# Mixture-of-experts front stage on one core: where z's scale and bias come from, and in what order its inputs are loaded

## What is computed

```
x_filtered = ifft(fft(x_quat, axis=1) * spectral_gate).real       # the gate is one factor per channel
x_rotated  = hamilton(normalize(cond), hamilton(x_filtered, conj(normalize(q_right))))
t      = x_rotated @ W_in + b_in
probs  = softmax(t @ W_gate + b_gate); topv, topi = top_k(probs, 2); topv = topv / sum(topv)
mid    = relu(einsum('nd,edh->neh', t, W1) + b1)                   # 8 experts, 256 -> 1024
eout   = einsum('neh,ehd->ned', mid, W2) + b2                      # 1024 -> 256
out    = x + (sum over the 2 choices of route * eout) @ W_out + b_out
```

## Time and profile before

| | |
|---|---|
| median of 3 runs | 515.55 us |
| the profiled execution | 515.1 us, of which the span of the profile is 513.2 us |
| granted TensorE clock | 1.00 |
| busy: TensorE, its weight loads, VectorE, ScalarE, GpSimd | 96%, 84%, 74%, 55%, 42% |
| chain that ended last | TensorE 83%, DMA 5%, issue 5%, VectorE 3%, ScalarE 2% |
| tile 0 starts | 79.69 us |
| second layer of the last tile ends | about 466 us |

### The profile page before, as it was taken

One profiled execution on the slowest core, in us unless ns is written; L12 is line 12 of the kernel. 1 busy time (PEld: TensorE's weight loads), 2 busy tenths in 40 slices (PEclk: granted clock), 3 DMA queues, 4 the chain that ended last, 5 costly groups with the idle time before them and its releaser, 6 DMA issues.

```text
span 513.2 us, 14538 instructions
## 1 busy us (share of the span) xinstructions
PE 494.9 (96%) x4658; PEld 430.7 (84%) x4659; DVE 380.6 (74%) x742; ACT 283.2 (55%) x576; POOL 217.5 (42%) x264
## 2 busy tenths in 40 slices
PE   7889998899999999999999999999899999999997
PEld 7556687788888888888888888889799999998786
DVE  4789987677786776878768787676568887864675
ACT  3533544655666556665566665336668778780221
POOL 4500025048456384464844637435545453321121
PEclk9999999999999999999999999999999999999999
DMA  6406534846556464555645543433354445133983
GB/s 225 158 2 209 190 125 124 237 143 205 139 172 188 140 213 131 164 179 155 198 144 163 175 122 93 115 100 99 91 163 150 135 130 150 34 114 126 406 333 140
DMA packets 75812, 80.62 MB, mean 157 GB/s; under 512 B 42983, under 2 KB 61740, under 8 KB 74732
## 3 DMA queue, kind: packets, MB, share of 16 engines
q1 hardware_dynamic: 56912, 41.44, 26.2%
q0 software_dynamic: 7936, 22.29, 13.0%
q10 hardware_dynamic: 10908, 16.17, 9.9%
HBM read 53.40 MB, written 26.48 MB: 156 GB/s over the span
## 4 chain that ended last, share of the span: by engine, by line
PE 83%; DMA 5%; issue 5%; DVE 3%; ACT 2%; ACTq 1%; SPq 0%; another core or an unknown queue 0%; DVEq 0%
PE bank L1399 24%; PE bank L1386 10%; PE bank L1325 8%; PE bank L1326 7%; PE bank L1327 7%; PE bank L1218 5%; PE bank L1455 5%; PE bank L1372 4%; PE bank L1374 4%; PE bank L1373 4%; DMA gq<-rows_by_slot 2%; DMA w1s<-y_by_choice 1%; PE bank L1465 1%; PE bank L1188 1%; DMA brow<-in_L_ffn_b_in 1%
## 5 line engine op out<-in xcount | busy, mean ns | idle before, releaser
L713 ACT ACTIVATE region<-bank,b1p,cbits 128x256 f32<-128x256 f32 (+1 forms) x368 | 163.1, 522 | 131.9 <-PE bank L1327 51.7
L567 POOL DMA_INDIRECT y_by_choice<-region,dst x71 | 87.3, 1229 | 166.9 <-DVE region L1063 151.5
L1399 PE MATMUL bank<-w2s,region 128*128 x1200 | 136.0, 273 | 0.9 <-issue 0.7
L1399 PEld LDWEIGHTS bank<-w2s,region 128*128 128x128 f16 x1200 | 116.7, 98 | 16.7 <-issue 2.9
L1094 DVE TENSOR_TENSOR region<-region 128x512 f16<-128x512 f32 (+1 forms) x184 | 104.0, 575 | 27.7 <-ACT region L697 20.4
L1325 PE MATMUL bank<-region,w1s 128*128 128x256 f16 x384 | 104.7, 273 | 4.3 <-DVE region L1100 2.2
L1327 PE MATMUL bank<-region,w1s 128*128 128x256 f16 x384 | 104.7, 273 | 0.0
L1326 PE MATMUL bank<-region,w1s 128*128 128x256 f16 x384 | 104.7, 273 | 0.0
L559 POOL DMA_INDIRECT region<-z_by_token,src x71 | 71.9, 1013 | 75.4 <-DVE src L1020 50.6
L1090 DVE CAST region<-region 128x512 f16<-128x512 f32 x100 | 46.0, 460 | 52.1 <-ACT region L713 47.9
L1372 PE MATMUL bank<-region 128*128 128x128 f16 x336 | 57.5, 219 | 1.1 <-DVE region L1100 0.5
(11 more groups left out here) (267 smaller groups left out, 644.4 us busy)
## 6 DMA issues: line engine op xcount, KB each, us to landing
region<-in_L_ffn_W ACTq DMA_DIRECT2D x14, 1024.0 KB
rows_by_slot<-region SPq DMA_DIRECT2D x33, 256.0 KB
gq<-rows_by_slot SPq DMA_DIRECT2D x132, 64.0 KB
w1s<-y_by_choice SPq DMA_DIRECT2D x12, 512.0 KB, 11.1
w1s<-in_x SPq DMA_DIRECT2D x8, 512.0 KB, 8.3
z_by_token<-w1s SPq DMA_DIRECT2D x16, 256.0 KB, 2.1
region<-in_L_ffn_W SPq DMA_DIRECT2D x2, 1024.0 KB
region<-in_x SPq DMA_DIRECT2D x8, 256.0 KB
```

What stands on the lines that cost most here:

```text
L567: g.indirect_dma_start(out=ybuf, out_offset=bass.IndirectOffsetOnAxis(ap=at, axis=0), in_=ysb[:, a % 2, h, :], in_offset=None).then_inc(s_ ...
L713: m = s.activation(midf[:, b, c * n:(c + 1) * n], FB[b][:, c * n:(c + 1) * n], ACT.Relu, bias=b1p[:, bass.ds(r, 1), f:f + 1].rearrange("p ...
L1399: last = mm(YB[par][:, h * D:(h + 1) * D], mids[:, par, l, b, c * TS + h * P:c * TS + (h + 1) * P], w2_at(e, w, f), start=(f == 0 and l == ...
```

## The change

- z's scale: the largest |x| squared, times 256, is replaced by the largest of the sums of squares of x over a group of x per partition. ScalarE makes these (`x_squares`, eight of them, with an accumulated sum), VectorE no longer makes maxima. `x_top` and `z_scale` stand later in VectorE's list, and their products later in TensorE's.
- `powers` and `expert_exponents` of the first expert stand behind the slot map.
- The bias matmul of each z pair is gone, with GpSimd's bias pieces. ScalarE copies the bias, in 128 rows, into the PSUM bank (`z_bias`), and the z matmuls add to it. For that TensorE first writes each of the five banks once.
- The first x groups are loaded first, from ACT's queue. Quaternions and gate are loaded as rows and transposed on TensorE. Four PSUM banks serve the transposes of x, not two. `wefft` comes from transposes of `weff`, no longer from a product of its own. The warm-up matmuls are 9, not 18; 4, 3 and 5 filler matmuls stand in the front.
- W1 is loaded in four DMAs of 256 columns each, so in runs of 1 KB, not 8 KB.

```diff
@@ loads
+            for half in range(2):
+                sp.dma_start(qrow[0:4, half, :], q_right).then_inc(s_q, 16)
+                sp.dma_start(qrow[4:4 + NCOND, half, :], cond).then_inc(s_q, 16)
+            load_x(sp, 2)
+            for half in range(2):
+                sp.dma_start(qrow[4 + NCOND:5 + NCOND, half, :], gate).then_inc(s_gt, 16)
+            for g in range(3, NG):
+                load_x(sp, g)
...
-                sp.dma_start(raw1[:], W1[bass.ds(e, 1)].rearrange("e (p k) f -> p (e k) f", p=P)).then_inc(s_w1, 16)
+                for c in range(4):
+                    sp.dma_start(raw1[:, :, c * CW:(c + 1) * CW], W1[bass.ds(e, 1), :, c * CW:(c + 1) * CW].rearrange(
+                        "e (p k) f -> p (e k) f", p=P)).then_inc(s_w1, 16)
@@ ScalarE
+            def x_squares(g):
+                act.wait_ge(s_x[g], 16)
+                s.activation(xsj[:, g], xin[:, g * XG:(g + 1) * XG].rearrange("p t d -> p (t d)"), ACT.Square,
+                             accum_out=xss[:, g:g + 1]).then_inc(s_xsq, 1)
+
+            load_x(act, 0)
+            load_x(act, 1)
+            act.dma_start(winr[:], W_in.rearrange("(k p) n -> p k n", p=P)).then_inc(s_win, 16)
...
+            s.activation(qsq[:, 14:16], ident[:, 0:2], ACT.Sqrt)
+            copy_xt(0)
...
+            copy_xt(1)
+            act.dma_start(binb[:, 0, :], b_in.partition_broadcast(P)).then_inc(s_binb, 16)
+            copy_xt(2)
             act.wait_ge(s_n2, 1)
             s.activation(nrm[:, 1, :], nrm[:, 0, :], ACT.Sqrt).then_inc(s_root, 1)
+            for i in range(2):
+                x_squares(i)
+            copy_xt(3)
             s.activation(nrm[:, 8, :], nrm[:, 0, :], ACT.Exp, scale=0.0)
...
+            for i in range(4, 11):
                 copy_xt(i)
+            x_squares(2)
             copy_logits(0)
+            for i in range(11, NP):
                 copy_xt(i)
...
+            for i in range(3, 5):
+                x_squares(i)
             copy_logits(1)
+
+            def z_bias(i):
+                if i >= NZ:
+                    act.wait_ge(s_zlo, i - NZ + 1)
+                else:
+                    act.wait_ge(s_zcl, i + 1)
+                s.activation(ZB[i % NZ][:].rearrange("p (t d) -> p t d", t=2), binb[:].to_broadcast([P, 2, D]), ACT.Copy
+                             ).then_inc(s_zb, 1)
+
+            act.wait_ge(s_binb, 16)
+            z_bias(0)
+            x_squares(5)
             exp(1)
+            for i in range(1, 3):
+                z_bias(i)
+            x_squares(6)
+            z_bias(3)
+            x_squares(7)
+            z_bias(4)
             act.wait_ge(s_sx, 1)
             act.wait_ge(s_wsq, 1)
             for i in range(NP):
                 z_out(i)
+                if 1 <= i <= NP - NZ:
+                    z_bias(i + NZ - 1)
@@ VectorE
-            z_scale()
+            dve.wait_ge(s_xsq, NG)
+            v.tensor_reduce(xss[:, NG:NG + 1], xss[:, 0:NG], AX.X, ALU.max).then_inc(s_xmx, 1)
             dve.wait_ge(s_rank, 1)
...
+            x_top()
...
             v.tensor_copy(order_i[:], cnt[:, 2, :]).then_inc(s_ord, 1)
+            z_scale()
...
-            powers(0, TB[1][:, 0:2])
-            expert_exponents()
             z_low(14)
             z_low(15)
...
+            powers(0, TB[1][:, 0:2])
+            expert_exponents()
             tile_ranks()
@@ TensorE
-            for i in range(18):
+            for i in range(9):
                 mm(bank[5][:, 0:P], ident[:], ident[:], start=True, stop=True)
+            pe.wait_ge(s_q, 16 * 4)
+            tr(bank[1][:, 0:NQ], qrow[0:NQ].rearrange("q h c -> q (h c)"), ident[0:NQ, 0:NQ]).then_inc(s_qp, 1)
...
-                if i >= NZ:
-                    pe.wait_ge(s_zlo, i - NZ + 1)
-                if i == NZ - 1:
-                    pe.wait_ge(s_sx, 1)
-                mm(ZB[i % NZ][:], ones3[:], bin3[:], start=True, stop=False, skip_group_check=True)
+                pe.wait_ge(s_zb, i + 1)
...
+            for i in range(3):
                 x_pair(i)
+            pe.wait_ge(s_gt, 16 * 2)
+            tr(bank[6][:, 0:1 + NQ], qrow[:].rearrange("q h c -> q (h c)"), ident[0:NQ + 1, 0:NQ + 1]
+               ).then_inc(s_gp, 1)
+            pe.wait_ge(s_brow, 16 * 2)
+            tr(bank[7][:, 0:NR], brow[:], ident[0:NR, 0:NR]).then_inc(s_btp, 1)
+            pe.wait_ge(s_const, 1)
+            spin(bank[5], 4)
...
-            for kd in range(KD):
-                for kj in range(KD):
-                    last = mm(bank[6][:, kd * D:(kd + 1) * D], winr[:, kj, kd * P:(kd + 1) * P], rt[:, kj, :],
...
+            for i in range(3, 7):
                 x_pair(i)
             pe.wait_ge(s_we, 1)
+            for ki in range(KD):
+                for kd in range(KD):
+                    last = tr(bank[6][:, kd * D + ki * P:kd * D + (ki + 1) * P], weff[:, ki, kd * P:(kd + 1) * P],
+                              ident[:])
+            last.then_inc(s_wtp, 1)
+            for i in range(7, 9):
+                x_pair(i)
+            pe.wait_ge(s_wt, 1)
...
             logits_half(1)
+            pe.wait_ge(s_ml, 1)
+            for i in range(NZ):
+                mm(ZB[i][:], ones16[:], iota16[:].rearrange("p c q -> p (c q)").unsqueeze(1).to_broadcast([P, 2, 2 * P]),
+                   start=True, stop=True).then_inc(s_zcl, 1)
             logits_t(1)
             z_pair(0)
             z_pair(1)
...
+            z_pair(2)
+            pe.wait_ge(s_xmx, 1)
+            tr(bank[7][0:1, 0:P], xss[:, NG:NG + 1], ident[:]).then_inc(s_xm1, 1)
+            z_pair(3)
+            (sums for z_scale)
+            for i in range(4, NP):
                 z_pair(i)
```

More of the change, by code:

```diff
@@ L63, in moe_program @@
         TB = [bank[i] for i in (2, 3)]
+        XTB = [bank[i] for i in (2, 3, 0, 4)]
         ZB = [bank[i] for i in (0, 1, 4, 6, 5)]
@@ L385, in combine, with load_x @@
                 step(i, i % 2)
[L388 to L399 removed]
+        def load_x(eng, g):
+            eng.dma_start(xin[:, g * XG:(g + 1) * XG], tokens(x_h, g * XG, XG)).then_inc(s_x[g], 16)
         @block.sync
         def _(sp):
[L403 to L406 removed]
+            for half in range(2):
[6 more added lines that the diff above has]
+                load_x(sp, g)
             sp.dma_start(wout[:], W_out.rearrange("(k p) n -> p k n", p=P)).then_inc(s_late, 16)
@@ L772, in _ @@
             link(last)
-            dve.wait_ge(s_q, 16 * 4)
+            dve.wait_ge(s_qp, 1)
             def row(first, rows, r):
-                t = qsrc[rows, first:first + 4].rearrange("p (c d) -> p c d", d=2)
+                t = bank[1][rows, first:first + 4].rearrange("p (c d) -> p c d", d=2)
                 return t[:, ::(-1 if r & 2 else 1), ::(-1 if r & 1 else 1)]
@@ L1175, in _, with spin @@
             pe.wait_ge(s_id, 1)
-            for i in range(18):
+            for i in range(9):
                 mm(bank[5][:, 0:P], ident[:], ident[:], start=True, stop=True)
-            pe.wait_ge(s_brow, 16 * 2)
-            tr(bank[7][:, 0:NR], brow[:], ident[0:NR, 0:NR]).then_inc(s_btp, 1)
+            NQ = 4 + NCOND
+            pe.wait_ge(s_q, 16 * 4)
+            tr(bank[1][:, 0:NQ], qrow[0:NQ].rearrange("q h c -> q (h c)"), ident[0:NQ, 0:NQ]).then_inc(s_qp, 1)
+            def spin(b, n):
+                for _ in range(n):
+                    mm(b[:, 0:2 * P], ones16[:], iota16[:].rearrange("p c q -> p (c q)"), start=True, stop=True)
             def x_pair(i):
@@ L1238, in _ @@
                 for kj in range(KD):
-                    mm(bank[1][:, ki * D:(ki + 1) * D], rt[:, kj, ki * P:(ki + 1) * P], winr[:, kj, :],
-                       start=(kj == 0), stop=(kj == KD - 1))
-            for kd in range(KD):
-                for kj in range(KD):
-                    last = mm(bank[6][:, kd * D:(kd + 1) * D], winr[:, kj, kd * P:(kd + 1) * P], rt[:, kj, :],
+                    last = mm(bank[1][:, ki * D:(ki + 1) * D], rt[:, kj, ki * P:(ki + 1) * P], winr[:, kj, :],
                               start=(kj == 0), stop=(kj == KD - 1))
             last.then_inc(s_wep, 1)
-            for i in range(2, 5):
+            for i in range(3, 7):
                 x_pair(i)
             pe.wait_ge(s_we, 1)
+            for ki in range(KD):
[6 more added lines that the diff above has]
+            pe.wait_ge(s_wt, 1)
             pe.wait_ge(s_small, 16 * 2)
@@ L1258, in _ @@
             mm(bank[7][:, 192:192 + E], ones[0:1, :], bgr[:], start=False, stop=True).then_inc(s_wgp, 1)
-            for i in range(5, 8):
+            for i in range(9, 11):
                 x_pair(i)
@@ L1289, in _ @@
             mm(TB[0][:, E * NT:2 * E * NT], ones16[:], m_et, start=True, stop=True).then_inc(s_rank, 1)
-            for i in range(2, NP):
+            z_pair(2)
+            pe.wait_ge(s_xmx, 1)
+            tr(bank[7][0:1, 0:P], xss[:, NG:NG + 1], ident[:]).then_inc(s_xm1, 1)
+            z_pair(3)
+            pe.wait_ge(s_xm2, 1)
+            pe.wait_ge(s_bsq, 1)
+            pe.wait_ge(s_wsq, 1)
```

(7 more changed lines are left out.)

127 lines of the change are left out of this document (39 added, 88 removed).

## The result

The changed kernel takes 522.87 us (median of 4 runs, 519.98 to 525.11) against 515.55 us for the kernel before beside it (514.03 to 517.0): the ratio is 1.0139, 95% interval 1.0078 to 1.0200. That is 7.3 us slower, above the predicted range. The profiled execution is the slowest of the four: it took 525.11 us, its span is 523.2 us.

A forecast was written before the change was run, and what follows sets the result against it. TensorE was taken as busy nearly throughout, with VectorE full too before the slot map. Front -2.0, middle +3.0, behind the slot map +0.2 and W1 0 gave +1.2, so 516.5 us, own range 514.2 to 518.0, eight in ten 512.4 to 519.8.

The forecast's parts named there:

- What bounds the kernel: Whole span: TensorE busy nearly throughout; only tile 0's start and tile 2's 2.2 us wait matter, other loop waits under 0.6.
- Front, -2.0: Up to the second half's logits at VectorE: they come at 29.6 instead of 31.6, 2.0 us gained.
- Middle, +3.0: From choices to slot map, 36.4 us before: VectorE's chain gets 3.0 us longer, bounds +0.8 and +4.5.
- Behind the slot map, +0.2: Slot map to tile 0: moved powers and exponents add 1.5 us, against 1.3 of slack, so +0.2.
- W1, 0 with bounds -2.2 and +1.0: W1's four loads in the tile loop: issues cost nothing, tile 2's gain is taken back; 0, bounds -2.2 and +1.0.
- Tile 2: Turned rows come at about 94, not 97.53; TensorE stops at W2's sum of squares instead, which doesn't move.
- Rival A: Slower: a low clock in the front makes tile 0 later, 517.8 us, or 520.5 if slow to 20 us; chance 0.36.
- B: Faster: ScalarE keeps ahead, middle costs only +0.8; 513.0 us, or 511.0 with tile 2; chance 0.22 together with C.
- C: Faster: the z pairs' bias matmuls were the bound, all 5.1 us count, 513 us; chance 0.22 together with B.

The follow-up runs named there:

- e7: The kernel before with W1 in two DMAs of 2 KB runs: 506.68 us, ratio 1.0005.
- e3: The kernel before with W1 in four DMAs of 32 whole partitions each, runs still 8 KB: 511.81 us, ratio 1.0129.
- e15: The kernel before with W1 in four short DMAs, issued by SyncE from the third expert on, the second expert's by ScalarE: 507.79 us, ratio 1.0034.
- e5: The kernel before, unchanged, traced on the same chip as e6: 508.16 us in its one run.
- e6: The changed kernel, unchanged, measured again on another chip: 514.08 us, ratio 1.0141.
- e1: The changed kernel with W1 of an expert as one DMA of 8 KB per partition again: 506.81 us, ratio 1.0044.
- e2: The kernel before with only W1 changed, to four DMAs of 1 KB runs for each expert: 513.47 us, ratio 1.0179.
- e10: The changed kernel, W1's issues from the third expert on spread behind relu pairs, expert's number read before each: 520.54 us, ratio 1.0181.
- e17: The changed kernel, W1's issues spread as in e10, but the expert's number read once: 510.46 us, ratio 1.0103.
- e8: The changed kernel with W1 in one DMA and the powers back between z_low(13) and z_low(14): 508.28 us, ratio 1.0034.
- e11: The kernel before with the second expert's W1 issued before the relus of tile 0: 514.08 us, ratio 1.0038.
- e14: The kernel before with W1 in four short DMAs, e2 again on another chip: 513.12 us, ratio 1.0142.
- e4: The changed kernel, W1 still short, with powers and exponents back between z_low(13) and z_low(14): 512.80 us, ratio 1.0165.
- e13: The kernel before, unchanged, traced on the same chip as e14 and e15: 505.27 us in its one run.
- e12: The changed kernel, W1 in one DMA, powers back, second expert's W1 issued before the relus of tile 0: 513.23 us, ratio 1.0024.

## Why the prediction was wrong

- **What bounds the kernel**: right for the stretch before tile 0, wrong in the conclusion that behind it only tile 2 mattered. "Nothing over 0.6 us" was read as room; it is a loop that is full (39.5 of 40 us), in which splits that come late by 2.35 us show, though those by 1.8 do not.
- **Front, -2.0**: right. 29.34 against a forecast of 29.6 (the items given there, 28.1 and 1.3, add up to 29.4); the scaled W_eff, due at 12.5, was begun at 12.50 and there at 13.25; the chain that ends in the logits runs through ScalarE's squares, copies and table load and not through it.
- **Middle, +3.0**: choices to slot map took 38.3 us (33.95 to 72.26), so +1.9, within its bounds. z_low(2) and z_low(5) wait 0.62 us each for ScalarE as written, TensorE has its waits of 1 to 2 us for bias writes. The wait for x_top was 1.02 us as written; that for the eighth square was 0.34 where I had 0.7, that for the sums 0.45 where I had 0.8.
- **Behind the slot map, +0.2**: wrong. I followed the chain back through the slot map, which released the gather before, and asked only what stands between it and tile 0. The gather also waits for all stores of z; in the kernel before these had landed by 72.97, and by how much is not shown, since a wait names its last releaser only. I had moved the powers away from between those z_low and costed the move on VectorE alone. Measured: slot map 0.4 earlier, tile 0 1.4 later, so +1.8.
- **W1, 0 with bounds -2.2 and +1.0**: this is the step that failed. Of its parts: the issues were taken at 0.4 us each (1.2 us more, from W1's 8 KB issue); with 1 KB runs they took 0.55 and the queue was held 2.35 us longer. They were compared with "a whole second layer (over 5 us)", TensorE's next need of ScalarE, and not with who really waits first, VectorE's splits. The runs put the cover between 1.8 and 2.35 us. The 1.2 us that I had would have cost next to nothing (e7 at 0.95, e3 at 1.45 us); the real length lay on the other side of the edge. The bound of +1.0 thought of packets only, and e15 shows that the packets were nearly harmless (1.0034). Size: the loop grew by 8.4 us in the first pair, 6.6 from e5 to e6, 7.0 from e1 to e6.
- **Tile 2**: half right. VectorE turned the rows without waiting for them and TensorE stopped at the sum of squares instead, as written. But they were turned at 97.54, not at about 94: VectorE came to them only then, behind splits that had waited 2.27 us for relus, which stood behind ScalarE's issues. And "the bytes are the same, so this doesn't move" left out that W2 and b2 stand behind W1's four issues: b2's issue went from 88.60 to 92.98, the square of W2 that waits for the landing from 99.34 to 102.29, and TensorE stood 2.72 us, then ran at a granted clock of 0.66 from 105 to 110 us.
- **Rival A**, the clock in the front: only its beginning came true. The granted clock is given as 1.00 up to 70 us, yet the first twelve transposes of x, from 6.70 us on, took 2.82 us where eight took 1.04 in the kernel before; the weights product, from 10.49, ran at the old pace. (The 1.7 in its price stands in no row; the earlier trace rows give 7 to 5.) The clock fell where no rival had looked: 0.93 from 70 to 80 us, with the stop for the gather, and behind the stop at the norms. **B and C**: no; TensorE's 5.1 us of bias matmuls came back as waits, 5.6 us of them, as in the forecast.
- The rest of the change without W1 is 1.0044 of before (e1), 2.2 us, with 1.4 to 3.1 for its interval; I had +1.2. With the powers back too it is 1.0034. No version tried here is faster than the kernel before.

**What stays open**: why W1 in four issues of long runs (e3) keeps TensorE 3.51 us at the second expert's norms, longer than four short ones (2.22 in e2); the trace shows W2's square waiting 3.41 us for its landing, not what held that up. And whether the stores of z could be brought off the gather's path without losing the earlier front was not tried beyond the powers' place.

## What to carry to other kernels

A DMA issue is an instruction on an in-order engine. When one DMA is cut into n, add up the issues as a hold of that engine, with the duration of the new shape, and follow the first instruction queued behind it to whoever waits for it, in the steady loop and not only at its worst wait. A loop that is full can have an edge: here a hold costs next to nothing up to 1.8 us, and 0.5 to 1.3 us for each of six loads from 2.35 us on. So two points on a trace say little, and a run with a pure hold on either side says much. If the cut is wanted, put the issues on a queue that idles, or between the engine's own instructions. And when the last releaser of a gather gets earlier, look up all of its semaphores: the next one is seldom far.

## What the runs showed of the hardware that I had not expected

- An issue's length depends on the shape, and not on bytes or on the run in HBM alone. W1's 1 MB with whole rows on both sides took 0.34 us; a quarter of it by partitions, still whole rows, 0.33; a half by columns (2 KB runs, strided on both sides) 0.57; a quarter by columns (1 KB) 0.55. W2's 1 MB, 1 KB runs in HBM but whole rows in SBUF, took 0.40.
- Reading the expert's number into a register takes 0.28 us of ScalarE's queue (median of 24 in e10; the longest anywhere, 0.77, stands at 91.22 in the kernel after), and the issue behind it begins some 0.6 us after the read does. The 0.8 us in what was expected of e17 is that longest one. Four reads in place of one are what e10 has over e17; their ratios are 1.0181 and 1.0103, but on different chips and with intervals that meet.
- The granted clock, which stood at the 2.4 GHz level, fell for some 5 us after single stops of TensorE of 2.6 to 4.0 us at tile 2 in the kernel after, e3, e6, e8, e10, e11, e14 and e17 (0.83 over 10 us, 0.66 in e3), and after two shorter ones in a row in e4 (1.43 and 2.15). It did not after 2.22 in e2, or 2.59 in e13, though it did after 2.57 in e10. The stop for the gather is 2.0 to 2.1 us in every version with the new front, and the clock from 70 to 80 us is 0.88 to 0.93 in the kernel after, e6, e10, e12 and e17, but 1.00 in e1, e4 and e8. So the length of a stop alone doesn't tell. In the kernel after, the 5 us from 105 hold 33 matmuls where 48 are usual, so the fall costs some 1.6 us on top of the stop's 2.7.
- The kernel before can have a slow front as well. In e5 the granted clock was 0.50, the 1.2 GHz level, from 20 to 25 us, and tile 0 starts at 81.40 instead of 78.93 in e13:

```profile
15.00:20.00 5.00, 3.88 (x29) 2.91 (x32) 4.93 (x10) 2.28 (x4) 4.41 (x8) 0.82 0.61 225
20.00:25.00 5.00, 5.00 (x26) 2.38 (x19) 1.54 (x2) 1.20 (x2) 2.24 (x4) 0.50 0.01 3
```

That is 2.5 us for no change in the program, as much as the 2.0 us that the change was to win in the front. e8, e11 and e14 had it too in their profiled executions (0.83, 0.66 and 0.66 from 15 to 25 us).
